# A decoder layer: low halves of the expert weights by accumulating DMAs, bias and mask rows folded on 80 partitions, new order lists

## The reference

```
x = layernorm(x + attn(x))    # gate = sigmoid(conv7(x)), cand = tanh(conv7(x)), per channel
                              # h[t] = decay * h[t-1] + gate[t] * cand[t]
                              # y = h @ out_w.T + out_b + x ;  y * rsqrt(mean(y*y)) * norm_w
x = layernorm(x + xattn(x, ctx))   # 16 heads of 8; q = x@Wq+bq, k = ctx@Wk+bk, v = ctx@Wv+bv
                              # causal scores q.k/sqrt(8) + attention_mask[k], softmax, @Wp + bp
x = layernorm(x + ffn(x))     # g = moe(x, w_gate), u = moe(x, w_up), silu(g)*u -> moe(., w_down)

def moe(x, router_w, expert_w):        # 8 experts, top 2, inner width 512
    vals, idx = top_k(x @ router_w.T, 2)
    combine   = softmax(vals) placed at idx, zero elsewhere
    return sum over e of combine[:, e] * (x @ expert_w[e].T)     # all 8 experts are computed
```

## Time and profile before

| | |
|---|---|
| median of 3 runs | 298.7 us (297.55 to 301.46) |
| profiled execution | 298.14 us, span 296.4 us |
| PE busy | 257.1 us, 87% of the span |
| DVE, POOL, ACT busy | 190.8, 111.1, 82.2 us |
| mean granted clock | 0.936 |
| the chain that ended last | PE 44%, DVE 31%, issue 12%, POOL 7%, ACT 3% |

### The profile page before, as it was taken

One profiled execution on the slowest core, in us unless ns is written; L12 is line 12 of the kernel. 1 busy time (PEld: TensorE's weight loads), 2 busy tenths in 40 slices (PEclk: granted clock), 3 DMA queues, 4 the chain that ended last, 5 costly groups with the idle time before them and its releaser, 6 DMA issues.

```text
span 296.4 us, 4809 instructions
## 1 busy us (share of the span) xinstructions
PE 257.1 (87%) x1756; PEld 188.2 (63%) x1756; DVE 190.8 (64%) x563; ACT 82.2 (28%) x157; POOL 111.1 (37%) x131
## 2 busy tenths in 40 slices
PE   6669857856986959999999999999999999999992
PEld 3546433425664737776777777777777787787871
DVE  5587862768697376556972884497188458566365
ACT  2424337135424201332133043114304313131000
POOL 4025329579314812048119205600930361070001
PEclk9997968995798885999999999999999999999997
DMA  5913625337420000262013005300300400320000
GB/s 192 380 50 112 197 75 148 116 106 214 160 71 1 3 0 0 109 209 77 0 48 107 2 0 170 125 0 13 142 2 1 155 0 2 71 81 9 2 0 18
DMA packets 12982, 23.48 MB, mean 79 GB/s; under 512 B 1584, under 2 KB 7824, under 8 KB 12954
## 3 DMA queue, kind: packets, MB, share of 16 engines
q1 hardware_dynamic: 11950, 22.17, 22.5%
q10 hardware_dynamic: 1008, 1.01, 1.0%
HBM read 19.81 MB, written 4.42 MB: 82 GB/s over the span
## 4 chain that ended last, share of the span: by engine, by line
PE 44%; DVE 31%; issue 12%; POOL 7%; ACT 3%; DMA 2%; SPq 1%; POOLq 0%; DVEq 0%; ACTq 0%
PE PS L1115 19%; PE PS L1167 8%; DVE NM L1321 4%; DVE ROOM L1454 3%; PE PS L1036 3%; PE PS L1047 2%; DMA PT<-aux 2%; DVE XL L1403 2%; PE PS L1050 2%; POOL PT L665 2%; DVE WL L1209 2%; PE PS L1010 2%; PE PS L881 2%; PE PS L1005 1%; PE PS L1089 1%
## 5 line engine op out<-in xcount | busy, mean ns | idle before, releaser
L1115 PE MATMUL PS<-WH,XH 128*128 128x512 f32 x128 | 57.8, 452 | 0.0
L1115 PE MATMUL PS<-WL,XH 128*128 128x512 f32 x128 | 52.2, 408 | 0.0
L1115 PE MATMUL PS<-WH,XL 128*128 128x512 f32 x128 | 52.2, 408 | 0.0
L689 POOL TENSOR_TENSOR ROOM<-ROOM,X2T 128x512 f32<-128x512 f32 x24 | 31.3, 1335 | 10.3 <-DMA ROOM<-CGD 10.3
L665 POOL TENSOR_SCALAR_AFFINE_SELECT PT<-PT 128x1024 f32<-128x1024 f32 x16 | 18.4, 1147 | 31.3 <-ACT PT L796 31.3
L1115 PEld LDWEIGHTS PS<-WH,XL 128*128 128x128 f32 x128 | 25.0, 196 | 6.1
L1115 PEld LDWEIGHTS PS<-WH,XH 128*128 128x128 f32 x128 | 25.1, 196 | 5.4 <-issue 0.4
L1115 PEld LDWEIGHTS PS<-WL,XH 128*128 128x128 f32 x128 | 25.2, 197 | 3.5 <-issue 0.2
L1167 PE MATMUL PS<-WH,ITH 128*128 128x512 f32 x56 | 23.7, 423 | 0.0
L607 POOL TENSOR_SCALAR R<-M 128x1 f32<-128x1 f32 x8 | 1.5, 190 | 58.0 <-DVE M L1467 58.0
L881 PE MATMUL PS<-XT,DIAG 128*128 128x256 f32 (+1 forms) x56 | 22.3, 538 | 0.0
(11 more groups left out here) (182 smaller groups left out, 491.8 us busy)
## 6 DMA issues: line engine op xcount, KB each, us to landing
ROOM<-CGD SPq DMA_DIRECT2D x12, 512.0 KB, 4.4
ROOM<-w_gate SPq DMA_DIRECT2D x4, 512.0 KB, 8.1
ROOM<-w_up SPq DMA_DIRECT2D x4, 512.0 KB, 4.5
ROOM<-w_down SPq DMA_DIRECT2D x4, 512.0 KB, 4.5
KD<-LOW SPq DMA_DIRECT2D x6, 256.0 KB, 4.4
KS<-KD SPq DMA_DIRECT2D x3, 512.0 KB, 3.6
QS<-QD SPq DMA_DIRECT2D x3, 512.0 KB, 4.5
QD<-LOW SPq DMA_DIRECT2D x3, 256.0 KB, 3.8
```

Source lines behind the costliest of these rows:

```text
L689: g.tensor_tensor(cb, cb, X2T[:, None, :].broadcast_to([P, 4, P]), ALU.mult).then_inc(f_xe, 1)
L1115: last = mm(PS[:, product_bank(t, r), :], a[:, r, cut], w[:, r, e * I:(e + 1) * I], start=e == 0 and n == 0, stop=e == E - 1 and n == 2)
```

## The change

1. **Low halves by DMA.** ACT makes WL = -WH (new step WN, line 743 of the changed kernel), then a DMA issued by POOL adds the weights from DRAM onto it (new step WA, line 639, `accum_op=ALU.add`). The steps WL of DVE and POOL are gone. RAW can be loaded anew after the cast. PE waits for the DMAs of a whole matrix.
2. **Rows on 80 partitions.** `aux` is loaded as 80 rows of 128 columns, split by two operations on ACT and one on DVE, stored to DRAM (AD) and loaded back from there on 5 rows into AUX; the mask rows go from AD to MD, and step MX of DVE is gone.
3. **New lists** EARLY and LATE and new places TILE_AT, SCALED_AT, PAIR_AT, SPAN, BRANCH_AT.

```diff
+A_FOLD = (A_T + M_COLS) // P
-TILE_AT = [1.0, 3.0, 2.0, 5.0, 10.0, 10, 10.5, 13.0, 13.0, 14.0, 17.0, 16.5, 17.5, 18.5, 24.0]
+TILE_AT = [-0.5, 3.5, 1.5, 5.0, 10.0, 10, 11.0, 13.0, 13.0, 13.5, 13.5, 16.5, 18.0, 24.5, 24.5]
...
+        AD = nc.dram_tensor("AD", (A_ROWS, A_FOLD * P), F32, kind="Internal").ap()
...
+            sp.dma_start(FOLD_RAW, aux.rearrange("a (c j) -> (a c) j", j=P)).then_inc(ld_a, 16)
             sp.dma_start(RO[:, :], rows.partition_broadcast(P)).then_inc(ld_r, 16)
-            sp.dma_start(AUX_RAW, aux).then_inc(ld_a, 16)
...
-                    sp.wait_ge(w_lo[c % WBUF], 2 * (c // WBUF))
+                    sp.wait_ge(w_hi[c % WBUF], c // WBUF)
                     sp.dma_start(RAW[:, c % WBUF, :], w_src[w][:, o:o + WCH]).then_inc(ld_w[c % WBUF], 16)
+                elif what == "AX":
+
+                    sp.wait_ge(c_aux, 3)
+                    sp.dma_start(AD.rearrange("a (c j) -> (a c) j", j=P), FOLD.bitcast(F32)).then_inc(st_a, 16)
+                    sp.wait_ge(st_a, 16)
+                    sp.wait_ge(c_id, 6)
+                    sp.dma_start(AUX[0:A_ROWS, :].bitcast(F32), AD[:, 0:A_COLS]).then_inc(ld_aux, 16)
                 elif what == "MX":
...
-                elif what == "WL":
-                    c, h = args
+                elif what == "WA":
+                    c, = args
                     w, o = chunk(c)
-                    o += h * WCH // 2
-                    pool.wait_ge(w_hi[c % WBUF], c // WBUF + 1)
-                    g.tensor_tensor(WL[:, w, o:o + WCH // 2], RAW[:, c % WBUF, h * WCH // 2:(h + 1) * WCH // 2],
-                                    WH[:, w, o:o + WCH // 2].bitcast(F32), ALU.subtract)\
-                        .then_inc(w_lo[c % WBUF], 1)
+                    pool.wait_ge(w_neg[c % WBUF], c // WBUF + 1)
+                    pool.dma_start(WL[:, w, o:o + WCH], w_src[w][:, o:o + WCH],
+                                   accum_op=ALU.add).then_inc(w_lo[w], 16)
...
+                elif what == "WN":
+                    c, = args
+                    w, o = chunk(c)
+                    act.wait_ge(w_hi[c % WBUF], c // WBUF + 1)
+                    s.activation(WL[:, w, o:o + WCH], WH[:, w, o:o + WCH].bitcast(F32), ACT.Copy, scale=-1.0)\
+                        .then_inc(w_neg[c % WBUF], 1)
                 elif what == "AX":
 
                     act.wait_ge(ld_a, 16)
...
+                    s.activation(FOLD_ALL, FOLD_RAW, ACT.Copy, scale=CO[0:A_ROWS * A_FOLD, C_AS:C_AS + 1])\
+                        .then_inc(c_aux, 1)
+                    s.activation(FOLD_LOW, FOLD_RAW, ACT.Copy, scale=CO[0:A_ROWS * A_FOLD, C_AW:C_AW + 1])\
+                        .then_inc(c_aux, 1)
...
                         pe.wait_ge(ld_k, NLK)
-                        pe.wait_ge(c_aux, 4)
+                        pe.wait_ge(ld_aux, 16)
...
                     if t == 0 and e == 0:
-                        for b, q in enumerate(w_lo):
-                            pe.wait_ge(q, 2 * chunks_in(b, CPW * (r + 1)))
+                        pe.wait_ge(w_lo[r], 16 * CPW)
...
-                            for q in w_lo:
-                                pe.wait_ge(q, 2 * NCH // WBUF)
+                            if t == 0:
+                                pe.wait_ge(w_lo[2], 16 * CPW)
...
-                    v.tensor_tensor(AUX[0:A_ROWS, :], AUX_RAW[:, 0:A_COLS], AUX_LOW[:, 0:A_COLS].bitcast(F32), ALU.subtract)\
-                        .then_inc(c_aux, 1)
+                    dve.wait_ge(c_aux, 2)
+                    v.tensor_tensor(FOLD, FOLD_ALL, FOLD_LOW.bitcast(F32), ALU.subtract).then_inc(c_aux, 1)
```

More of the change, by code:

```diff
@@ L42 @@
 C_AW = C_AS + 1
-C_AM = C_AW + 1
-C_BK, C_BQ = C_AM + 1, C_AM + 2
+C_BK, C_BQ = C_AW + 1, C_AW + 2
 NCOL = C_BQ + 1
@@ L70 @@
+LATE = {'ACT': [(4.5, ('W', 11)), (2.7, ('WN', 9)), (7.699999999999999, ('WN', 11)), (2.0, ('W', 10)), (0.5, ('W', 9)), (2.2, ('WN', 10)), (-3.0, ('W', 8)), (0.7000000000000002, ('WN', 8))], 'DVE': [], 'POOL': [(1.2999999999999998, ('WA', 10)), (10.8, ('WA', 11)), (2.3000000000000003, ('WA', 9)), (1.3000000000000007, ('WA', 8))], 'SP': [(-5, ('W', 7)), (13.5, ('W', 8))]}
 TURNED = 2
-TILE_AT = [1.0, 3.0, 2.0, 5.0, 10.0, 10, 10.5, 13.0, 13.0, 14.0, 17.0, 16.5, 17.5, 18.5, 24.0]
-SCALED_AT = [23.0, 28.5, 33.0, 35.0, 35.0, 36.5, 38.0, 41.5, 44.0]
@@ L73 @@
-PAIR_AT = [8.5, 9.0]
-SPAN = {1: (-2.5, 6.5), 2: (7.0, 23.5)}
-BRANCH_AT = [-3.5, 7.5, 11.0, 13.0, 15.5, 16.9, 19.0]
+TILE_AT = [-0.5, 3.5, 1.5, 5.0, 10.0, 10, 11.0, 13.0, 13.0, 13.5, 13.5, 16.5, 18.0, 24.5, 24.5]
+SCALED_AT = [22.5, 30.5, 31.5, 32.5, 35.5, 35.0, 37.5, 44.0, 45.0]
+PAIR_AT = [6.5, 7.0]
+SPAN = {1: (-1.5, 6.5), 2: (7.0, 23.5)}
+BRANCH_AT = [-13.5, 6.0, 8.0, 8.5, 15.4, 16.5, 18.5]
 def tile_plan(t):
@@ L323, in decoder_layer @@
         c_aux = sem("c_aux")
+        st_a = sem("st_a")
+        ld_aux = sem("ld_aux")
         dv = sem("dv")
@@ L560, in _ @@
                     if t == TURNED:
-                        for split in w_lo:
-                            sp.wait_ge(split, 2 * NCH // WBUF)
+                        for split in w_hi:
+                            sp.wait_ge(split, NCH // WBUF)
                         sp.wait_ge(f_t, 4 * TURNED)
@@ L1203, in _ @@
                 what, args = x[0], x[1:]
-                if what == "WL":
-                    c, h = args
-                    w, o = chunk(c)
-                    o += h * WCH // 2
-                    dve.wait_ge(w_hi[c % WBUF], c // WBUF + 1)
-                    v.tensor_tensor(WL[:, w, o:o + WCH // 2], RAW[:, c % WBUF, h * WCH // 2:(h + 1) * WCH // 2],
-                                    WH[:, w, o:o + WCH // 2].bitcast(F32), ALU.subtract)\
-                        .then_inc(w_lo[c % WBUF], 1)
-                elif what == "GC":
+                if what == "GC":
                     j, *taps = args
@@ L1233, in _ @@
                 elif what == "AX":
-                    dve.wait_ge(c_aux, 3)
-                    dve.wait_ge(c_id, 6)
-                    v.tensor_tensor(AUX[0:A_ROWS, :], AUX_RAW[:, 0:A_COLS], AUX_LOW[:, 0:A_COLS].bitcast(F32), ALU.subtract)\
-                        .then_inc(c_aux, 1)
-                elif what == "MX":
-                    dve.wait_ge(c_aux, 4)
-                    v.tensor_tensor(MASKS, AUX_RAW[:, A_T:A_T + M_COLS], AUX_LOW[:, A_T:A_T + M_COLS].bitcast(F32),
-                                    ALU.subtract).then_inc(c_aux, 1)
+                    dve.wait_ge(c_aux, 2)
+                    v.tensor_tensor(FOLD, FOLD_ALL, FOLD_LOW.bitcast(F32), ALU.subtract).then_inc(c_aux, 1)
                 elif what == "RD":
@@ L1499, in marks @@
         return np.isin(row, which).astype(np.float32)[:, None]
+    row_of, part = np.arange(P) // A_FOLD, np.arange(P) % A_FOLD * P
+    scales = np.where((row_of < 2) & (part >= A_Q) & (part < A_T), np.float32(SCALE), np.float32(1))
+    lows = (row_of == np.where(part < A_T, 1, 4)).astype(np.float32)
     cols = np.concatenate([
@@ L1504 @@
         marks(*range(2, 32, COPIES)), marks(*range(1, 32, COPIES), MASK_LO),
-        np.where(np.arange(P) < 2, np.float32(SCALE), np.float32(1))[:, None],
-        (np.arange(P) == 1).astype(np.float32)[:, None],
-        (np.arange(P) == 4).astype(np.float32)[:, None],
+        scales[:, None], (scales * lows)[:, None],
         a["L0_xattn_bk"][:, None], a["L0_xattn_bq"][:, None]], axis=1)
```

22 lines of the change are left out of this document (7 added, 15 removed).

## The result

The changed kernel takes **288.7 us** (median of four runs, 286.86 to 291.06), the kernel before 299.18 beside it (four runs). The ratio is 0.970, with a 95% interval of 0.964 to 0.976: 3.0% faster. Some executions of every kernel here run slower at a lower clock; the ratios and their intervals leave these out, the medians do not. The forecast was 287.0 with a range of 279 to 301. The profiled execution is the slowest of the four, 291.06 us with a span of 289.3, so I show beside it the same kernel run once more (e5: 287.13, span 285.4).

The account below looks back on a forecast made before the run. PE bounds the kernel, with winnable idle time up to 118 us, mostly waits for DVE. 10.7 us by IT-0 plus 1.5 from the clock make 12.2, less 1.1 for overlooked waits: 298.1 - 11.1 = 287.0, range 279 to 301.

Parts of the forecast that it names:

- Part 1: Bias and mask rows, 0 to 32 us: K's product 2.7 us later, first scores 0.4 us later.
- Part 2: Attention of tile 0, 32 to 57 us: exponentials start at 42.8, selects run 43.9 to 46.1, 4.0 us earlier.
- Part 3: To the first T and G, 57 to 78 us: gain 3.4 us at XE-0, T-1 1.6 earlier, tile 1's selects 4.0 earlier.
- Rival 2: ACT takes DVE's place, busy 19.5 of 32 us from 40 to 72; Part 2 and Part 3 give nothing: 295, chance 0.12.
- The accumulating DMA: Weights' low halves: landing taken as 9 us (3.9 to 18.4), POOL's issue as 1.2 (0.33 to 9.2); hidden, costing nothing.
- estimate of 4.4 us for a landing: Skill's DMA formula, about 2.0 us plus 2 x 512 KB at 436 GB/s; the sum would stay the same.
- Part 4: Tiles 1 and 2, 78 to 110 us: ST-2-0 about 8.3 us earlier; with 2.4 off GATE's wait, IT-0 10.7 earlier.
- Part 5: Clock from 110 to 118 us and the rest: 1.5 us gained (bounds 0 and 4); after 118, 0 (-2 to +2).
- Rival 1: The clock recovers too: all 4 us of 110 to 118 and 3 of the stretch at 0.57; 280.4, chance 0.10.
- Rival 3: DVE and POOL hold each other up: seven issues on the path each held 0.86 us, 6 us go: 293, chance 0.10.
- estimated 304.5: Skill's two-port DVE mode delays GpSimd's descriptor writing, 3.1 us instead of 0.62: result if 2.5 us are lost seven times.
- Rival 4: POOL held by seven issues ahead of T and X: gain gone at 2.8 us each, 313.6 with 5; chance 0.12.

Follow-up runs that it names:

- e7: Changed kernel without its twelve accumulating DMAs, so low halves are not computed and PE waits for the negations: 290.82 us, ratio 0.974.
- e9: Changed kernel with w_up's negations and accumulating DMAs and VM-1 put behind expert inputs, and second-half maxima ahead of T-0 on DVE: 294.2 us, ratio 0.988.
- e12: e9 with two of w_up's four accumulating DMAs (WA-4, WA-6) and their negations back ahead of the expert inputs: 286.19 us, ratio 0.961.
- e1: Kernel before with only the changed kernel's five place tables; weights, rows, EARLY and LATE as before: 298.09 us, ratio 0.995.
- e8: Changed kernel with only BRANCH_AT taken from the kernel before: 295.14 us, ratio 0.986.
- e2: Changed kernel with the five place tables of the kernel before; accumulating DMAs, folded rows, EARLY and LATE stay new: 296.53 us, ratio 1.002.

## Why the prediction was right, and where not

The time was right and the sign too, through errors that cancel.

- **Part 1, the store behind the chunks**: right (forecast K at 19.5, was 18.8). "The first scores start 0.4 us later": **failed**, 2.3. The step counted the wait and not the clock after it (4.4 us for K instead of 2.4).
- **Part 2, 4.0 us for tile 0's attention**: mis-sized. The selects ended at 47.5 us instead of 50.08, 2.6 earlier, because the exponentials began at 44.23 and not at 42.8: the 2 us of part 1 came in here. What PE made of it hung on the clock: PV-0 1.5 later or 1.1 earlier.
- **Part 3, 3.4 at XE-0, T-1 1.6 earlier**: **failed**. XE-0 came 2.5 later (0.3 earlier in e5), T-1 4.6 later (1.7 in e5). The step put the wait for WN-5 and WA-5 too low and left out that VM holds up DV. Rival 2 (ACT takes DVE's place) came true in part, at T-1; but ACT was busy 13.69 us from 40 to 72, not the 19.5 that it counted.
- **The accumulating DMA**: right in size. Landing 5.8 to 11.1 us, median 7.7, for 9 taken; POOL's issue 0.86 to 1.54 us for 1.2 taken. The estimate of 4.4 us for a landing was under the fastest. No cost seen, by e7. But what they ask of the DMA engines was counted at half: twelve are 13.0% of 289.3 us, 3.1 us each, and eight 25 us, not 13. "Without that cover KS and QS of tile 2 come late" is what e9 then did, and e12 undid.
- **Part 4, DVE without low halves**: the waits went as forecast, the time did not. (4.0, 1.3 and 2.9 make 8.2; the sum carried 8.3.) From G-0-0 to ST-2-0, before and then after:

```profile
72.10:93.65 21.55, 16.70 (x138) 12.54 (x136) 18.56 (x43) 7.48 (x13) 7.99 (x8) 0.87 0.33 98
```

```profile
73.70:93.95 20.25, 19.00 (x146) 13.85 (x144) 16.80 (x36) 10.88 (x18) 10.32 (x12) 0.78 0.85 183
```

  PE's idle time fell from 4.85 to 1.25 us, 3.6 for 4.2 counted. But its busy time rose by 2.3: the eight matmuls of ST-1-1 stand behind G-0-0 now (1.1 us), and the clock is 0.78 instead of 0.87. That is the step of the sum that failed here: it put PE's work at the same length. GATE: 2.4 counted, 2.6 measured: right, and for the reason given (e1, e8).
- **Part 5, the clock**: 1.5 counted, 3.3 measured from IT-0 to L-0; the upper bound of 4 was nearer. Later tiles: 0 counted within 2 either way, 1.4 to 2.0 measured. A tile takes 25.5 us instead of 25.8 (mean of L-1 to L-4), in e1 as well (25.5) and not in e2 (25.8): it is the places, not the new operations.
- **Rival 1**, that the clock recovers too: half of it. From 110 to 118 us yes, at 66 to 78 no (0.62, in e5 0.50, before 0.57).
- **Rival 3, DVE and POOL hold each other up**: one way only. POOL's issues were not held. DVE was, as the last section shows, mostly off the path but at DV on it. By the Trainium skill (SBUF — State Buffer, the "DVE blocks DMA" trap and the section behind it) an issue beside a DVE copy can take 3.1 us, for an estimated 304.5; no issue of the changed kernel took over 1.54 and none of any run over 1.83, so the measurement decides against it for this kernel.
- **Rival 4, POOL held by the issue**: fell. At 0.86 to 1.54 us the point from which it decides, 2.8, is far.

Where the gain is from, then: 2.6 us from a shorter wait for GATE and 3.3 from the clock that this wait used to cost, both from the places of BRANCH_AT (e8), most likely from its norm ahead of U-0-0. With the old operations the new places gave nothing clear of the noise (e1), with the new operations and the old places nothing came either (e2). The other 1.4 to 2.0 come from the places in the later tiles, and 3 more where the clock at 44 us holds. Why the executions of one kernel differ there is open.

## What to carry to other kernels

Price a wait of PE with the work behind it at the lower clock: here 3.6 us of waiting cost another 3.3, and 4.6 cost 2 more. Test the two halves of a change that moves work off an engine and uses the room: each alone may show nothing. And before a hidden DMA is put off, look whose load it will then share the DMA engines with: two issues 7 us later went with 8 us more, 5 of them one wait for a load.
